# Gated delta attention on one core: taps read from PSUM, a shorter refinement of the inverse, sums of squares from an accumulator, and new orders on all engines

## The reference

```python
mixed = silu(causal_conv(hidden @ W_qkvz.T, conv_w, taps=4))     # q, k, v
q, k  = l2norm(q), l2norm(k)
g = cumsum(g in chunks); decay = exp(g_i - g_j) for i >= j
A = -strict_tril((k*beta) @ k.T * decay)
T = inverse of (eye - A)                                          # lower triangular
value_ = T @ v_beta ;  k_cumdecay = T @ (k_beta * exp(g))
for chunk in chunks:
    v_new = value_ - k_cumdecay @ state
    out   = (q * exp(g)) @ state + (q @ k.T * decay) @ v_new
    state = state * exp(g_last) + k_dec.T @ v_new
out = rmsnorm(out) * silu(z) @ W_out.T
```

## Time and profile before

| | |
|---|---|
| median of 3 runs | 5350.27 us (5350.02 to 5354.16) |
| the profiled execution, its span | 5350.3 us |
| PE busy | 4982.9 us, 93% |
| DVE busy | 4483.8 us, 84% |
| ACT busy | 4371.8 us, 82% |
| POOL busy | 2064.9 us, 39% |
| granted PE clock between 2000 and 4500 us | 1.00 |

### The profile page before, as it was taken

How to read it: one execution, slowest core, us unless ns; L and a number is a source line. 1 busy time by engine, 2 the same in 40 slices (tenths; PEclk the granted TensorE clock), 3 DMA queues, 4 the chain that set the end, 5 groups by cost and what they waited for, 6 DMA issues and landing times. The chain is left out here.

```text
span 5350.3 us, 132947 instructions
## 1 busy us (share of the span) xinstructions
PE 4982.9 (93%) x38788; PEld 3326.6 (62%) x38788; DVE 4483.8 (84%) x9152; ACT 4371.8 (82%) x9744; POOL 2064.9 (39%) x1433
## 2 busy tenths in 40 slices
PE   5899999999999999999999999999999999999978
PEld 3566666666666666666666666666666666666644
DVE  4888888888888888888888888888888888888853
ACT  3788888888888888888888888888888888888842
POOL 2344434344443434444344444434444343444410
PEclk7999999999999999999999999999999999999988
DMA  3222212121121212212121221212122121221112
GB/s 141 75 63 63 75 62 81 60 70 69 62 81 60 79 60 72 71 62 77 60 82 61 65 74 62 81 59 74 65 66 77 60 79 60 72 70 62 64 65 82
DMA packets 185165, 377.26 MB, mean 71 GB/s; under 512 B 86400, under 2 KB 95744, under 8 KB 184960
## 3 DMA queue, kind: packets, MB, share of 16 engines
q1 hardware_dynamic: 185088, 376.46, 21.8%
HBM read 360.13 MB, written 16.25 MB: 70 GB/s over the span
## 5 line engine op out<-in xcount | busy, mean ns | idle before, releaser
L653 PE MATMUL p_proj<-hid,w_in 128*128 128x512 f32 x3072 | 1620.5, 610 | 32.4 <-POOL ident L1163 29.7
L998 DVE SCALAR_TENSOR_TENSOR conv<-pre,taps,conv 128x512 f32<-128x512 f32 x1536 | 1207.8, 793 | 41.9 <-ACT conv L857 37.6
L911 ACT ACTIVATE x_bd<-x_t 64x512 bf16<-64x512 bf16 x1280 | 804.5, 629 | 215.7 <-DVE x_t L1079 198.9
L1205 POOL TENSOR_TENSOR o_sc<-o_sc,neg_half 128x8 f32<-128x8 f32 x128 | 268.6, 2099 | 1622.0 <-DVE o_sc L1135 1622.0
L653 PEld LDWEIGHTS p_proj<-hid,w_in 128*128 128x128 f32 x3072 | 496.6, 192 | 64.5 <-POOL ident L1163 30.0
L838 PE MATMUL p_out<-h_t,w_out 128*128 128x512 f32 x1024 | 501.9, 613 | 0.8 <-DVE h_t L1140 0.8
L1072 DVE TENSOR_TENSOR y_h<-p_lev,y_h 128x512 bf16<-128x512 f32 x640 | 441.3, 690 | 44.2 <-PE p_lev L707 37.9
L1116 DVE TENSOR_TENSOR vw<-p_b,w_c 128x256 f32<-128x256 f32 x384 | 156.9, 409 | 378.8 <-PE p_b L796 378.8
L1079 DVE STREAM_TRANSPOSE x_t<-y_h 128x512 bf16<-128x512 bf16 x640 | 454.6, 710 | 19.3
L1064 DVE TENSOR_TENSOR q_h<-p_lev,consts 128x512 bf16<-128x512 f32 x640 | 438.6, 685 | 37.9 <-PE p_lev L701 33.3
L1172 POOL TENSOR_TENSOR low<-g_row,consts 128x1024 f32<-128x1024 f32 x128 | 302.1, 2360 | 410.1 <-ACT dec L895 409.9
(11 more groups left out here) (210 smaller groups left out, 12168.4 us busy)
## 6 DMA issues: line engine op xcount, KB each, us to landing
w_in<-in_w_in SPq DMA_DIRECT2D x128, 768.0 KB, 6.2
g_row<-rows_scratch SPq DMA_DIRECT2D x128, 512.0 KB, 3.1
hid<-h_scratch SPq DMA_DIRECT2D x128, 512.0 KB, 7.3
e_row<-exp_rows_scratch SPq DMA_DIRECT2D x128, 512.0 KB, 5.1
w_out<-in_w_out SPq DMA_DIRECT2D x128, 256.5 KB, 2.6
x<-in_x SPq DMA_DIRECT2D x8, 512.0 KB, 10.4
h_scratch<-x SPq DMA_DIRECT2D x8, 512.0 KB, 2.6
y_scratch<-y_acc SPq DMA_DIRECT2D x8, 512.0 KB, 5.6
```

The source lines that it names most:

```text
L653: last = pe.matmul(p_proj[tile % 2][:], w_in[p][:, kt, tile * P:(tile + 1) * P], hid[p][:, kt, :], start=(kt == 0), stop=(kt == KT - 1))
L911: last = act.activation(x_bd[block, :, block], x_t[block], ACT.Copy)
L998: dve.scalar_tensor_tensor(conv[:, tile, :], pre[:, tile, j:j + S], taps[p][:, tile, j:j + 1], conv[:, tile, :], ALU.mult, ALU.add).then_i ...
```

## The change

1. The buffer `pre` goes. C writes `conv` alone, and the T tasks read `p_proj` at a shift. A bank of `p_proj` is now free for tile n+2 when the third T of tile n is done.
2. The refinement has one residual in place of two. D multiplies `y_dn` by A in three bf16 parts: the upper halves of the fp32 `ga` read in place (`top`, every second bf16 element), the upper halves of `a_rest`, and `a_lo`. F (DVE) adds the identity and writes the residual `resid` in fp32. G (PE) and v (ACT) make `g_t` from it, RL (POOL) makes `r_lo`, and W adds `x_dn` and three products for each unit. d, N, n, E and e go. `a_rest` is made by AR, a new POOL task.
3. AD goes. AB reads `ga` in fp32; AO (ACT) copies one 64x64 block of A for Q6. Z6 and XC take all 128 partitions.
4. KN and QN (ACT) square chunk by chunk and take the sums from the accumulator; the sums on DVE go.
5. p6 moves from DVE to ACT.
6. All four orders are written anew. PE, DVE and POOL now reach four steps ahead instead of three. GE stands right behind YC on ACT, before XC.

```diff
-                    act.activation(pre[:, n, PAD:], p_proj[n % 2][:], ACT.Copy)
                     act.activation(conv[:, n, :], p_proj[n % 2][:], ACT.Copy, scale=taps[p][:, n, PAD:PAD + 1])\
...
-                    dve.scalar_tensor_tensor(conv[:, tile, :], pre[:, tile, j:j + S], taps[p][:, tile, j:j + 1],
-                                             conv[:, tile, :], ALU.mult, ALU.add).then_inc(s[f"tap{tile}"], 1)
+                    late = PAD - j
+                    dve.scalar_tensor_tensor(conv[:, tile, late:], p_proj[tile % 2][:, 0:S - late],
+                                             taps[p][:, tile, j:j + 1], conv[:, tile, late:], ALU.mult, ALU.add)\
...
-                        t.wait(pe, "pre_done", tile - 1)
+                        t.wait(pe, f"tap{tile - 2}")
...
-                    act.activation(squares[:, 0], bank(0), ACT.Square).then_inc(s["k_sq"], 1)
+                    for c in range(NC):
+                        last = act.activation(squares[:, 0, c, :], bank(0)[:, c, :], ACT.Square, accum_out=sums[:, 0, c:c + 1])
...
-                        pe.matmul(bank(n)[:, u - n * 4, :], a_d[:, u, :], y_dn[:, u, :], start=True, stop=False)
+                        pe.matmul(bank(n)[:, u - n * 4, :], top(ga[p][:, u, 0, :]), y_dn[:, u, :], start=True, stop=False)
+                        pe.matmul(bank(n)[:, u - n * 4, :], top(a_rest[:, u, :]), y_dn[:, u, :], start=False, stop=False)
                         last = pe.matmul(bank(n)[:, u - n * 4, :], a_lo[:, u, :], y_dn[:, u, :], start=False, stop=True)
...
-                        pe.matmul(bank(n)[:, u - n * 4, :], f0[:, u, :], x_dn[:, u, :], start=False, stop=False)
-                        last = pe.matmul(bank(n)[:, u - n * 4, :], f1[:, u, :], x_dn[:, u, :], start=False,
+                        pe.matmul(bank(n)[:, u - n * 4, :], r_lo[:, u, :], x_dn[:, u, :], start=False, stop=False)
+                        pe.matmul(bank(n)[:, u - n * 4, :], top(resid[:, u, :]), x_dn[:, u, :], start=False, stop=False)
+                        last = pe.matmul(bank(n)[:, u - n * 4, :], top(resid[:, u, :]), g_t[:, u, :], start=False,
...
+                elif name == "F":
+                    t.wait(dve, "d_mm", n + 1)
+                    t.wait(dve, "w_mm", n + 1, back=1)
+                    t.wait(dve, "rlo", back=1)
+                    dve.tensor_tensor(quarter(resid, n), bank(n), each(const["ident"], 4), ALU.add).then_inc(s["r_done"], 1)
...
+                elif name == "AR":
+                    pool.tensor_tensor(a_rest[:], ga[p][:, :, 0, :], tops(ga[p][:, :, 0, :]), ALU.subtract).then_inc(s["rest"], 1)
...
+                elif name == "RL":
+                    pool.tensor_tensor(r_lo[:], resid[:], tops(resid[:]), ALU.subtract).then_inc(s["rlo"], 1)
```

More of the change, by code:

```diff
@@ L759, in emit @@
                     for u in range(n * 4, n * 4 + 4):
-                        last = pe.matmul(bank(n)[:, u - n * 4, :], x_dn[:, u, :], f0[:, u, :], start=True, stop=True)
-                    last.then_inc(s["n_mm"], 1)
-                elif name == "E":
-                    t.wait(pe, "n_done", n + 1)
-                    t.wait(pe, "strict")
+                        last = pe.matmul(bank(n)[:, u - n * 4, :], top(resid[:, u, :]), x_dn[:, u, :], start=True, stop=True)
+                    last.then_inc(s["g_mm"], 1)
+                elif name == "W":
+                    t.wait(pe, "g_done", n + 1)
+                    t.wait(pe, "rlo")
@@ L765, in emit @@
                     if n == 0:
[L766 to L774 removed]
+                        t.wait_newest(pe, (0, ("g_done", 1)), (2, ("y_added", 1)), (-1, ("ga_done", 2)),
+                                          (0, ("r_done", 1)), (-1, ("k_tok_done", None), ("k_sq", None)),
+                                          (0, ("v_tok_done", 1)), (2, ("h_done", 1)), (1, ("inv_done", 1)))
+                    else:
+                        t.wait_newest(pe, (1, ("h_done", None)), (0, ("g_done", None)), (2, ("y_added", None)),
+                                          (-1, ("ga_done", None)), (0, ("r_done", None)), (-1, ("q_sq", None)),
+                                          (0, ("v_tok_done", None)), (1, ("inv_done", None)))
@@ L888, in emit @@
                     t.wait(act, "qt_mm")
-                    t.wait(act, "q_sum", back=1)
-                    act.activation(squares[:, 1], bank(1), ACT.Square).then_inc(s["q_sq"], 1)
+                    t.wait(act, "q_sq", back=1)
+                    t.wait(act, "rooted", back=1)
+                    for c in range(NC):
+                        last = act.activation(squares[:, 1, c, :], bank(1)[:, c, :], ACT.Square, accum_out=sums[:, 1, c:c + 1])
+                    last.then_inc(s["q_sq"], 1)
                 elif name == "GE":
@@ L920, in emit @@
                     t.wait(act, "d_mm", back=1)
-                    t.wait(act, "n_done", back=1)
                     act.activation(y_dn[HB:P, :, 0:HB], p_lev[HB:P, :].rearrange("p (u f) -> p u f", f=HB), ACT.Copy)\
                        .then_inc(s["y21"], 1)
+                elif name == "p":
+                    t.wait(act, "q6_mm")
+                    t.wait(act, "z6_mm", back=1)
+                    act.activation(p_h[HB:P], p_lev[HB:P, :].rearrange("p (u f) -> p u f", f=HB), ACT.Copy)\
+                       .then_inc(s["p6_done"], 1)
                 elif name == "XC":
@@ L1046, in emit @@
                         t.wait(dve, "o_mm", back=2)
-                        t.wait(dve, "e_mm", back=2)
+                        t.wait(dve, "d_mm", back=2)
                     for h in range(HD):
@@ L1154, in _ @@
                 pool.sem_inc(counted, SPARE * counts[name])
-            for tile in (a_bd, x_bd, y_dn):
+            for tile in (a_bd, a_off, x_bd, y_dn, p_h):
                 pool.memset(tile[:], 0.0)
-            pool.memset(pre[:], 0.0)
             pool.memset(y_acc[:], 0.0)
```

193 lines of the change are left out of this document (99 added, 94 removed), and 3 rows, old and new, of the table DVE_ORDER.

## The result

The changed kernel takes 4987.03 us, the median of 4 runs (4986.47 to 4992.39). The kernel before took 5350.15 us beside it. The ratio is 0.9325, with a 95% interval of 0.9312 to 0.9338. The forecast was 5112 us: right in its direction and inside its range, 125 us too slow. The gain is 363 us where 238 were forecast, and the time lies only 2 us inside the faster end of the stretch (4985 to 5228 us) that the prediction had called the forecast.

What follows compares the result with a forecast made beforehand. Bound: a chain of handoffs closing on itself each turn, no engine full. YC to GA 4.45 + GA to L 5.75 + L to YC 27.0 = 37.2 us, 1.86 less, times 128 = 238: 5350.3 - 238 = 5112 us; range 4970 to 5300.

Steps and rivals of the forecast that it cites:

- A chain from YC to YC: Loop turn: handoffs from engine to engine, closing on themselves one turn later, set its 39.06 us; no load does.
- the walk: The chain followed through the new orders, each instruction starting at the later of its engine and releaser: turn 37.2 us.
- W: Theory of one chain of handoffs: an instruction counts whole where it stands in the chain and nothing elsewhere.
- YC to GA: From the last piece of y_dn to the first GA: 7.64 us falls to 4.45, with GE right behind YC.
- GA to L: From the first GA to the start of the next inverse: 7.92 us falls to 5.75, without AD before AB.
- L to YC: From the start of the next inverse through its levels to YC: 23.50 us grows to 27.0, walked 26.8.
- x_dn, QN (1.4) and YC on ACT 4.1: Last term of L to YC, after XD: 4.1 us on ScalarE, QN 1.4 of it.
- T from PSUM: VectorE's T, reading PSUM and SBUF, avoids the stall beside POOL's ON: 0.74 us each, 0.6 us a turn back.
- The price of the alternative: If T could still meet POOL's passes, the 0.6 us wouldn't come back: some 80 us over the loop at most.
- Strided bf16 weights: Rival on PE: 40 weight loads a turn at a step of two elements cost up to 3.7 us, 5490; slower 0.05.
- GE behind YC: ScalarE order: GE right behind YC makes YC to GA 0.59 + 1.28 + 2.44 and 0.15 for handoffs, 4.45 us.
- The banks held by the taps: Slower rival: p_proj banks free only after three T, PE waits on late T, turn 40.2 us, 5490; chance 0.09.

Runs made afterwards that it cites:

- ge_behind_xc: The changed kernel with XC done ahead of GE on ScalarE, as in the kernel before, the rest of its order kept: 5126.24 us, ratio 0.9579.
- top_parts_only: The changed kernel with D using only the top bf16 part of the strict blocks and W only that of the residual: 4985.45 us, ratio 0.9321.
- p6_on_dve: The changed kernel with p6 back on VectorE, between RR3 and SN1: 5017.87 us, ratio 0.9379.
- whole_squares: The changed kernel with KN and QN squaring a whole bank in one instruction and VectorE summing right ahead of SM0: 4983.23 us, ratio 0.9312.
- whole_squares_f_first: The changed kernel with KN and QN squaring whole banks, sums on VectorE, and F0 ahead of SM0 there: 4934.91 us, ratio 0.9230.
- vx_on_dve: The changed kernel with the last vx copy of a turn moved from ScalarE to VectorE and F0 ahead of SM0: 4953.14 us, ratio 0.9259.
- taps_from_sbuf: The changed kernel with ScalarE making the four plain projection copies again and T reading them in SBUF instead of PSUM: 5397.08 us, ratio 1.0086.
- l_first: The changed kernel with both AB right behind GA3, L between OY0 and OY1, and M1 ahead of W0: 5289.91 us, ratio 0.9885.
- before_ge_early: The kernel before with GE right behind YC on ScalarE, ahead of the d copies and XC: 5867.65 us, ratio 1.0971 to the kernel before.
- pad_outside: The changed kernel with one unused extra ScalarE copy ahead of SV0, outside its unbroken stretch: 5016.32 us, ratio 0.9375.
- pad_inside: The changed kernel with one unused extra ScalarE copy ahead of SK, inside its unbroken stretch: 5076.03 us, ratio 0.9488.

## Why the prediction was right, and where it was off

**The bound.** A chain from YC to YC set the turn, as said, and not a load: ge_behind_xc moves GA by 1.06 us and the turn by 1.07, top_parts_only takes 24 products a turn from TensorE and gains nothing. It is right with two reservations: the gain was forecast a third too small, and two of the three pieces came near their figures by errors that cancel. What the walk didn't see is how many chains lie within 0.5 us of it in the new orders. For that p6_on_dve and whole_squares went against W, and of the runs only those that shorten one chain and keep the next from growing (whole_squares_f_first, vx_on_dve) gave time.

**The pieces.** Each mark as it lies in the trace, means over the turns of the window:

| piece | predicted | measured |
|---|---|---|
| YC to GA | 4.45 | 4.56 |
| GA to L | 5.75 | 5.56 |
| L to YC | 27.0 (walked 26.8) | 26.2 |

YC to GA came as walked: YC, the table load and `dec` end at 4.35 us, and GA follows. GA to L is near its figure by terms that cancel: SL ends at 4.49, as said; AB follows after 0.15 us where 0.4 was put, the two AB take 0.87 and not 0.7, and L follows within 0.06.

The three leave 0.9 us a turn, 111 of the 125 us; the rest lies outside the loop, which I had left as it was. Within L to YC, L to M1 took 1.79 instead of 1.35, since M1 stands behind W0, which waits 0.70 us for `g_t`. M1 to Y1 was 2.2 for 2.6, so that Y1 came where it was said to, 4.0 us behind L, and that was luck: what holds Y1 is XB1, behind X1 on DVE and behind IV0 on ACT, and the walk on record names no IV0. From Y4 to Y5 it was 5.6 for 5.2. The others were within 0.2. Together the terms up to XD measured 0.4 us more than walked. **The term that was mis-sized is the last, "x_dn, QN (1.4) and YC on ACT 4.1": it measured 3.15.** QN took 1.00 from the start of its first piece to the start of the next instruction. The row of OQ is the time in which an OQ runs, 2.75 us for eight; they stand in pairs, and the end of each second one, during which the next instruction already runs, is in it. The pieces follow one another at about 0.29 us, QN's at 0.25. That is 0.4 of the 0.95 us. How the other 2.7 us of the term were split isn't on record; they measured 2.15: 0.8 from XD to `x_dn`, 0.9 to QN, 0.4 for the vx copy. The 0.2 us that I had added to the walk weren't needed either.

**T from PSUM.** T is at 744 ns, with ON, AR, AL, RL and SL beside it, against 792; as said. The price of the alternative was put far too low: 0.6 us a turn, some 80 us at most, and 40 to 80 us expected of taps_from_sbuf. It is 277 us in the new orders, plus 133 for the copies. Without this part the changed kernel, its orders otherwise as they are, is slower than the one before.

By the Trainium skill (SBUF — State Buffer, section SBUF: two separate sides) whichever comes first of a VectorE instruction with two SBUF inputs and a GpSimd one that reads SBUF holds the ports for its whole length. The rows of 1998.96 and 1999.10 agree.

What failed in the 80 us is the count of the stalls. T meets not one or two passes of GpSimd in a turn but three to four, and not only the new ones: its own time grows by 2.7 us a turn.

**The other costs.** Strided bf16 weights load in 98 ns, as packed ones; that rival falls. (Half of its 3.0 us would have given a turn of 38.7 us, not 38.9.) AB takes 418 ns where I took 350. It isn't covered: AB starts only when SL has ended, and L starts 0.06 us behind AB, in l_first too, where TensorE waits for AB alone. So the two AB cost some 0.17 us a turn more than put, an estimate from 0.87 against 0.70 us. POOL has 18.2 us a turn, not 20.2: AR, AL and RL take 1894 to 1896 instead of 2140 ns, 0.7 us together, and three small passes (PW 1647 instead of 2085 ns, the power in OP 1742 instead of 2106, the product behind it 202 instead of 652) make 1.3. ACT (31.75 for 31.5) and DVE (31.3 for 31.5) are as worked out. PE fell by 2.4 us, not 1.1; it didn't matter.

**GE behind YC.** Right, and it was only possible with the rest: in the kernel before the same move costs 519 us, because the refinement's copies of d on ACT come late and TensorE's clock falls while it waits for them. AB without AD and XC behind GE were right too; RL ended well ahead of W0.

**The banks held by the taps.** Right to call it the slower rival and unlikely here: no P waits for a T. But it is near. One more copy on DVE brings 0.5 us of such waits a turn, and stalled T bring 1.1.

**Part 4 of the change** (the sums from the accumulator) is worth nothing as laid out here, -4 us when undone. The fastest version has it undone, with F0 ahead of SM0; F0 ahead with part 4 kept and nothing else changed wasn't run.

Left open: how the 2.2 us of taps_from_sbuf are shared between the bank and the levels; how much of the gain the new refinement brings by itself, and the orders by themselves, since the pieces depend on each other. The kernel before with T reading PSUM in its old orders wasn't tried.

## What to carry to other kernels

When a schedule has been packed by hand, look for the second wait behind the first: the releaser named ahead of the instruction that starts late (here GA, first `dec`, then KK) changes as soon as one chain is shortened, and time comes only when both are. An in-order engine that waits on something early (`neg_n` for PW) holds ready work behind it; moving the ready work ahead gave 1% for nothing. Before a VectorE instruction gets a second input in SBUF, count in the new order how many passes of GpSimd it will stand beside: here twelve such instructions a turn met three to four, and 2.2 of the 2.7 us of stalls went into the turn. And a wait that two rows show, that of a weight load and that of the product behind it, is one wait.

## What the runs showed of the hardware

- T with both inputs in SBUF meets GpSimd's passes in both directions: T (the 128x510 ones) 970 instead of 744 ns in the mean and 2.30 us in the worst case, `a_lo` 2338 instead of 1896 ns, the select of SL 1521 instead of 1098.
- A bf16 weight load that takes every second element takes 98 ns, like a packed one.
- Squares with a sum from the accumulator follow one another at 0.25 us for a piece of 128 columns: four pieces take 1.00 us, where one plain square of 512 columns takes 0.59.
- The copy from fp32 to bf16 of 64x512 within SBUF took 418 ns, from PSUM 695 ns.
- ScalarE pauses 1.3 to 1.5 us in every second turn, at one place in a loop whose body is two turns (pad_outside; 1.5 to 2.0 us in pad_inside).
- With TensorE busy 0.52 of 2 us, its granted clock was 0.63 and 0.52 over the next 4 us (before_ge_early, 0.93 over the loop).
